# Keys, values and queries as three products of high and low parts in the rounded 32-bit type, single input buffers, a ring of 10 rows

## What is computed

```python
q = layernorm(x) @ Wq + bq;  k = ctx @ Wk + bk;  v = ctx @ Wv + bv
qp = elu(q) + 1;  kp = elu(k) + 1
# causal: sums over s <= t of kp[s] (outer) v[s], times qp[t], for each head
out = (cumulated(kp v) . qp) / cumsum(qp, axis=1)
x = x + out @ Wo + bo
h = relu(layernorm(x) @ W1 + b1);  sel = argmax(h @ W2 + b2)
x = x + layernorm(x) @ expert_W[sel] + expert_b[sel]
```

## Time and profile before

| | |
|---|---|
| time, median of 3 runs | 1251.42 us (1249.2 to 1252.38) |
| span of the profiled execution | 1101.6 us |
| the profiled execution's own time | not given apart from its span; the median is 149.8 us longer than the span |
| PE, DVE, POOL, ACT busy | 1010.6, 879.8, 672.5, 374.5 us |
| one full step | 30.70 us |

### The profile page before, as it was taken

How to read it: one execution, slowest core, us unless ns; L and a number is a source line. 1 busy time by engine, 2 the same in 40 slices (tenths; PEclk the granted TensorE clock), 3 DMA queues, 4 the chain that set the end, 5 groups by cost and what they waited for, 6 DMA issues and landing times.

```text
span 1101.6 us, 37703 instructions
## 1 busy us (share of the span) xinstructions
PE 1010.6 (92%) x15724; PEld 723.6 (66%) x15724; DVE 879.8 (80%) x1908; ACT 374.5 (34%) x581; POOL 672.5 (61%) x578
## 2 busy tenths in 40 slices
PE   1869999999999999999999999999999999997683
PEld 1446666666777776776677777776676767776472
DVE  2468888998988988888988888888998888885552
ACT  0323333333333343343333333344333333331220
POOL 5134556555666666677666666677766566565755
PEclk9979999999999999999999999999999999998887
DMA  4743434444455445555555544445555544351451
GB/s 139 232 113 101 125 121 125 126 128 145 130 163 160 137 121 145 153 150 164 137 153 163 158 120 126 152 150 163 144 148 165 151 120 128 102 151 41 160 174 53
DMA packets 90920, 152.52 MB, mean 138 GB/s; under 512 B 19325, under 2 KB 57856, under 8 KB 90624
## 3 DMA queue, kind: packets, MB, share of 16 engines
q1 hardware_dynamic: 68864, 107.82, 35.3%
q0 software_dynamic: 12672, 33.84, 8.4%
q10 hardware_dynamic: 9216, 8.46, 3.7%
HBM read 98.20 MB, written 36.13 MB: 122 GB/s over the span
## 4 chain that ended last, share of the span: by engine, by line
PE 78%; DVE 8%; issue 4%; DMA 2%; SPq 1%; POOL 0%; ACT 0%; DVEq 0%; POOLq 0%; ACTq 0%
PE b_a L916 23%; PE b_b L921 18%; PE b_s L1006 9%; PE b_b L953 6%; PE b_s L930 6%; PE b_b L963 5%; DVE stage L634 3%; PE b_s L943 3%; PE b_s L971 2%; PE b_a L911 2%; PE b_s L991 2%; DVE kp L783 1%; DVE st L769 1%; DVE vsel L790 1%; DMA out<-rows 1%
## 5 line engine op out<-in xcount | busy, mean ns | idle before, releaser
L634 DVE TENSOR_TENSOR stage<-b_s,causal 128x1024 f32<-128x1024 f32 x192 | 225.5, 1215 | 6.7 <-PE b_s L930 4.2
L466 POOL DMA_INDIRECT out<-rows x136 | 160.3, 1178 | 45.1 <-issue 34.6
L458 POOL DMA_INDIRECT buckets<-row,place x128 | 141.6, 1106 | 34.5 <-issue 34.2
L916 PE MATMUL b_a<-x_T,wq_sb 128*128 128x512 f32 x256 | 128.9, 628 | 18.7 <-POOL x_T L483 14.2
L475 POOL TENSOR_TENSOR onehots<-onehots,onehot 128x32 bf16<-128x32 bf16 x32 | 7.8, 243 | 193.7 <-DVE place L754 193.7
L921 PE MATMUL b_b<-wo_sb,attT 128*128 128x256 f32 x512 | 121.3, 391 | 2.9 <-DVE attT L831 2.9
L916 PE MATMUL b_a<-ctxT,wk_sb 128*128 128x512 f32 x256 | 118.4, 605 | 1.8 <-ACT pos L530 1.8
L921 PE MATMUL b_b<-wv_sb,ctxT 128*128 128x256 f32 x512 | 119.0, 386 | 0.0
L483 POOL TENSOR_TENSOR x_T<-x_T,scale 128x1024 f32<-128x1024 f32 x32 | 75.5, 2360 | 65.6 <-DMA scale<-scales 64.8
L1006 PE MATMUL b_s<-we_sb,x3T 128*128 x464 | 113.2, 389 | 1.0 <-ACT x3T L539 1.0
L497 POOL TENSOR_TENSOR x_res<-x_res,bias_o 128x1024 f32<-128x1024 f32 x32 | 105.8, 3305 | 5.7 <-DMA x_res<-in_x 5.5
(11 more groups left out here) (125 smaller groups left out, 1794.2 us busy)
## 6 DMA issues: line engine op xcount, KB each, us to landing
rows<-buckets SPq DMA_DIRECT2D x136, 130.0 KB
x_in<-in_x SPq DMA_DIRECT2D x32, 512.0 KB, 4.1
x_T<-in_xT SPq DMA_DIRECT2D x32, 512.0 KB, 4.0
ctxT<-in_ctx SPq DMA_DIRECT2D x32, 512.0 KB, 4.6
qsel<-qp SPq DMA_DIRECT2D x256, 64.0 KB, 2.4
x_res<-in_x SPq DMA_DIRECT2D x32, 512.0 KB
scale<-scales ACTq DMA_DIRECT2D x32, 256.0 KB, 3.9
out<-rows POOLq DMA_INDIRECT x136, 3.4
```

The source lines that it names most:

```text
L458: pool.indirect_dma_start(buckets, bass.IndirectOffsetOnAxis(place[:, slot(route), t:t + 1], 0), row[:, slot(route), t, :], None).then_inc ...
L466: pool.indirect_dma_start(out.rearrange("t p n -> (t p) n"), bass.IndirectOffsetOnAxis(rows2[:, r, TOKEN:TOKEN + 1].bitcast(U32), 0), rows ...
L634: dve.tensor_tensor(dst.rearrange("p g h s q -> p g (h s) q"), b_s[:, :, 256 * t:256 * t + 256].rearrange("p g (a q) -> p g a q", q=C), ca ...
L916: last = pe.matmul(dst, w[:, k, P * h:P * h + P], rows[:, k, :], start=(k == 0), stop=(k == KC - 1))
```

## The change

The weights Wq (after its mean is taken out), Wk and Wv, the scaled x_T and ctxT are each split into a high part, the value rounded to float32r by an ACT copy, and a low part, the value minus the high part, also rounded. Each product becomes three: high x high, high x low, low x high. The low parts of x_T and ctxT are made by POOL, those of the weights once by DVE. To make room, x_in, x_res and ctxT have one buffer, attT and x2n share one, the plain weights lie in `stage` until they are split, and the ring of rows has 10 places instead of 15. The diff, cut to its core:

```diff
-    RING = 15
+    RING = 10
...
-    MADE = 13
+    MADE = 19
...
+        wq_parts = [sb(f"wq_{part}", [P, KC, D], F32R) for part in ("high", "low")]
...
-        x_in = sb("x_in", [P, 2, GT, D])
-        x_res = sb("x_res", [P, 2, GT, D])
-        ctxT = sb("ctxT", [P, 2, KC, N])
+        x_in = sb("x_in", [P, GT, D])
+        x_res = sb("x_res", [P, GT, D])
+        ctxT = sb("ctxT", [P, KC, N])
+        ctx_parts = [sb(f"ctx_{part}", [P, KC, N], F32R) for part in ("high", "low")]
...
+        x_parts = [sb(f"x_{part}", [P, KC, N], F32R) for part in ("high", "low")]
...
-        attT = sb("attT", [P, KC, N])
+        att_or_x2n = sb("att_or_x2n", [P, KC * N])
...
+        wq_sb, wk_sb, wv_sb = (stage[:, KC * D * i:KC * D * (i + 1)].rearrange("p (k n) -> p k n", k=KC) for i in range(3))
...
@@ sync: step
-                    if group_no(load) >= 2:
-                        sp.wait_ge(s_st1, n(load, 4, -4))
+                    if group_no(load) >= 1:
+                        sp.wait_ge(s_st1, n(load, 4))
...
-                    if group_no(norm) >= 2:
-                        sp.wait_ge(s_v, n(norm, 2, -2))
+                    if group_no(norm) >= 1:
+                        sp.wait_ge(s_clow, n(norm))
...
-                        sp.wait_ge(s_x1, added)
+                        sp.wait_ge(s_x1, n(attend, 2))
...
-                        sp.wait_ge(s_q, n(load, 2))
+                        sp.wait_ge(s_xlow, n(load))
...
@@ gpsimd
+            def x_low(norm):
+                pool.wait_ge(s_xhigh, n(norm, k=1))
+                if group_no(norm) >= 1:
+                    pool.wait_ge(s_q, n(norm, 2))
+                pool.tensor_tensor(x_parts[1][:, :, :], x_T[:, :, :], x_parts[0][:, :, :], ALU.subtract).then_inc(s_xlow, 1)
...
                     pool.tensor_tensor(z[:, :], z[:, :], u[:, :], ALU.mult).then_inc(s_zprod, 1)
+                    if norm:
+                        x_low(norm)
...
                     pool.tensor_tensor(rstd1[:, :], ve1[:, :], column(neg_half), ALU.pow).then_inc(s_rstd1, 1)
+                if norm:
+                    pool.wait_ge(s_chigh, n(norm, k=1))
+                    pool.tensor_tensor(ctx_parts[1][:, :, :], ctxT[:, :, :], ctx_parts[0][:, :, :], ALU.subtract)\
+                        .then_inc(s_clow, 1)
...
@@ scalar
+            for parts, w in ((wk_parts, wk_sb), (wv_parts, wv_sb)):
+                act.activation(parts[0][:, :, :], w, ACT.Copy).then_inc(s_whigh, 1)
+            act.wait_ge(s_cst, MADE - 6)
+            act.activation(wq_parts[0][:, :, :], wq_sb, ACT.Copy).then_inc(s_whigh, 1)
...
+                if norm:
+                    act.wait_ge(s_xs, n(norm, k=1))
+                    if group_no(norm) >= 1:
+                        act.wait_ge(s_q, n(norm, 2))
+                    act.activation(x_parts[0][:, :, :], x_T[:, :, :], ACT.Copy).then_inc(s_xhigh, 1)
                 turn_out(extra_slots_of(j))
...
                     first_queries(norm, 1)
+                    act.wait_ge(s_ctx[slot(norm)], 16 * half(norm) + 16)
+                    if group_no(norm) >= 1:
+                        act.wait_ge(s_v, n(norm, 2))
+                    act.activation(ctx_parts[0][:, :, :], ctxT[:, :, :], ACT.Copy).then_inc(s_chigh, 1)
...
@@ vector
+            for at, (parts, w) in enumerate(((wk_parts, wk_sb), (wv_parts, wv_sb), (wq_parts, wq_sb))):
+                dve.wait_ge(s_whigh, at + 1)
+                for k in range(KC):
+                    dve.tensor_tensor(parts[1][:, k, :], w[:, k, :], parts[0][:, k, :], ALU.subtract).then_inc(s_cst, 1)
             dve.wait_ge(s_cst, MADE)
...
@@ tensor
+            def pairs_of_parts(weights, rows):
+                for k in range(KC):
+                    for a, b in ((0, 0), (0, 1), (1, 0)):
+                        yield weights[a][:, k, :], rows[b][:, k, :], k == 0 and a + b == 0, k == KC - 1 and a == 1
+            def channels_first_parts(dst, weights, rows, h):
+                for w, r, start, stop in pairs_of_parts(weights, rows):
+                    last = pe.matmul(dst, w[:, P * h:P * h + P], r, start=start, stop=stop)
+                return last
...
-                    pe.wait_ge(s_ctx[a], 16 * half(project) + 16)
+                    pe.wait_ge(s_clow, n(project, k=1))
                     pe.wait_ge(s_qe, n(project, 4, 4))
-                    channels_first(b_a[:, 0, :], wk_sb, ctxT[:, a, :, :], 0).then_inc(s_k, 1)
+                    channels_first_parts(b_a[:, 0, :], wk_parts, ctx_parts, 0).then_inc(s_k, 1)
...
-                        last = tokens_first(b_b[:, t // 2, D * (t % 2):D * (t % 2) + D], ctxT[:, a, :, :], wv_sb, t)
+                        last = tokens_first_parts(b_b[:, t // 2, D * (t % 2):D * (t % 2) + D], ctx_parts, wv_parts, t)
...
-                    pe.wait_ge(s_xs, n(norm, k=1))
+                    pe.wait_ge(s_xlow, n(norm, k=1))
...
-                    channels_first(b_a[:, 0, :], wq_sb, x_T, 0).then_inc(s_q, 1)
+                    channels_first_parts(b_a[:, 0, :], wq_parts, x_parts, 0).then_inc(s_q, 1)
```

More of the change, by code:

```diff
@@ L5 @@
 F32 = mybir.dt.float32
+F32R = mybir.dt.float32r
 BF16 = mybir.dt.bfloat16
@@ L485, in step @@
                                        ALU.mult).then_inc(s_xs, 1)
+                if norm and not attend:
+                    x_low(norm)
                 if merge and j < STEPS - 2:
@@ L817, in step @@
                     for t in range(GT):
-                        dve.bn_stats(st1[:, t, :], x_in[:, slot(load), t, :]).then_inc(s_st1, 1)
+                        dve.bn_stats(st1[:, t, :], x_in[:, t, :]).then_inc(s_st1, 1)
                     aggregate1(load)
```

42 lines of the change are left out of this document (25 added, 17 removed).

## The result

| | before | after |
|---|---|---|
| time, median | 1250.47 us (1249.2 to 1252.38, 4 runs) | 1265.23 us (1259.85 to 1275.29, 4 runs) |
| ratio | | 1.0131, 95% interval 1.0081 to 1.018 |
| profiled execution: its time, its span | span 1101.6 | 1269.16, 1267.4 |

The account below looks back on a forecast made before the run. PE was taken to bound the steps, with a POOL and DVE loop closing after the change. Steps +7 - 3, fill +10 and tail +31 gave +45, 1296 us, rounded down to 1294; range 1263 to 1335.

Parts of the forecast that it names:

- +7 - 3 = +4: Steps: 24 full ones +0.3 us each, +7; six or so earlier ones gain about 0.5 each, -3.
- so I set the sum against the span and take what lies around it as unchanged: Starting point: 149.8 us of the 1251.42 us median lie around the 1101.6 us profiled span and stay unchanged.
- (a): Rival: POOL's path is shorter, PE's gain arrives in full, 28.0 us steps, 1211 us, 5%; half the gain, 1261, 5%.
- (d): Rival: the shorter ring doesn't slow the tail, as its loads are covered; 1263 us, 4%.
- POOL's loop: Steps: POOL's list with two subtractions, closed through DVE from onehots to onehots, takes 30.8 to 31.2 us against 30.70.
- PE's 2.8 us a step: Projections on PE: rounded products at a quarter price give 2.8 us less work a step, which turns into waits.
- x_res without the scan in its way: POOL in a step: x_res, reached 3 us later, no longer meets the DVE scan and takes 2.36 us, not 3.62.
- Fill +10: Before the first rank product: weight parts on DVE +2.7 us, copies and subtractions before first queries and keys +6.8, together +10.
- Tail +31: Tail with ring of 10: +8 us from loads delaying the pad stores, +23 from five of seven quads waiting.
- first pair of products 1.75: Tail: PE's first pair of products priced at 1.75 us, half of 3.49, within 9.8 us a quad.
- (b): Rival: a POOL subtraction costs like x_res, 3.6 us, lengthening the loop by 2.4 us more; 1363 us, 12%.
- (c): Rival: rounded products cost half of a 32-bit product on PE, +5.6 us a step; 1420 us, 4%.

Follow-up runs that it names:

- the ring alone: Kernel before with a ring of 10 rows instead of 15 and nothing else; 1146.47 us, ratio 1.0374.
- high parts alone: Changed kernel with only the high x high product, low parts of x and context neither made nor multiplied; 1107.09 us, repeated at 1103.73.
- half of the late sums: Kernel before with late sums over the first half of the positions only; 1081.01 us, ratio 0.9777, repeated at 1079.37.
- the queries first: Kernel before with the first half of the queries ahead of the first late sums on PE; 1116.85 us, ratio 1.0094.
- Single buffers (+2.1%): Kernel before with one buffer each for x_in, x_res and ctxT, nothing else changed; 1276.24 us, ratio 1.0209.
- plain products: Changed kernel with all its splitting, but one plain 32-bit product of the high parts for each three; 1172.55 us (1.0612) and 1277.83 us (1.0198).

## Why the prediction was wrong, and where it was right

Rank products mark the stages. From their rows (first and last start) and the spans:

| | first rank product | from first to last | to the end |
|---|---|---|---|
| forecast | +10 | +7 - 3 = +4 | +31 |
| first kind (109.2, 927.7, 69.7 to 114.8, 938.8, 108.7) | +5.6 | +11.1 | +39.0 |
| second kind (105.7, 1060.0, 80.9 to 116.1, 1037.9, 113.4) | +10.4 | **-22.1** | +32.5 |

**The step that failed** is "so I set the sum against the span and take what lies around it as unchanged". Nothing but 1.7 us lies around the span. The profiled execution and the timed runs were made, as far as the spans tell, on two kinds of chip, and on the one that was timed the steps take 36 us, not 30.70. There the working starts from a wrong bound: PE's work stretched by pauses among its small products, 5.2 us a step. From the first rank product to the last the change saves 22 us there, where the forecast had +4. The same block averages, before against after, show of what: a step falls from 36.3 to 34.4 us. The small products take 1.0 us less (early scores -1.0, late sums -3.8, early sums +3.7), keys, values and queries 2.2 less, of which 1.2 is in the first queries, and PE waits 1.0 longer ahead of the late sums, for vsel. So the pauses moved more than they shrank, and PE's cheaper projections, which the forecast saw turn into waits, show here in part. Fill and tail came near the forecast, +43 together against +41. In sum the traces have +20.8 us (1267.4 - 1246.6), the medians +14.8, the forecast +45. It is luck that 1265 lies in the range and beside the times of two rivals, the half of (a) at 1261 and (d) at 1263: (d) has the tail unchanged, which it isn't, and the half of (a) counts from steps of 30.7 us without pauses. A gap of 12% between span and median called for a rival of its own: that the timed runs have other steps than the profiled one.

**On the kind of chip that the rows came from, most of the working held.** Its sum was +45, measured +58 by the medians (1162.61 - 1104.32), +55.7 by the traces. Not shown is that POOL's loop alone sets the steps: with x_low taken out of it they stayed at 31.5 us, on a chain through DVE and PE. Point by point there:

- Rounded products at a quarter: right, a start every 0.23 us for 512 columns. The forecast's sign of being wrong, "records of the rounded products over 0.25 us", would have misled: the records last 0.40 us and overlap. PE's 2.8 us a step: PE's busy time fell from 30.52 to about 29, not to 28; the gain went into waits, as forecast, some of them for vsel, which the forecast took to be there in time (29.3 us over the run).
- ctx_low at 2.46: 2.36 measured. x_low at 2.46 behind kp: mean 2.77, as it waits for kp's end.
- Steps of 30.8 to 31.2: 31.0 to 31.3 in those without a table, 31.9 in those with one. On the mean of steps 12 to 25 it is 31.6 against 31.1 in the kernel before, +0.5 instead of +0.3. The term is too small, and what the rows show beside it is the second query sum, which x_res now meets; the forecast had "x_res without the scan in its way" and did not follow whom it meets in its new place.
- POOL's idle ahead of onehots "from 6 to about 2 us": 2.22.
- Fill +10: +5.6 on this kind, +10.4 on the other.
- Tail +31: +37.7 by the ring alone. The two parts were +8 and +23; measured, the first of the 28 blocks is sent 31.0 us after the last rank product (1068.79 - 1037.8) instead of 24.2, +6.8, and the 28 take 67.1 instead of 35.5 us, +31.6. The largest miss is in "first pair of products 1.75": 3.0 to 3.4 with part of it at the lower clock. A turn takes 11 us instead of 9.8, and the first two 13.6 and 11.8.
- Single buffers at nothing: agrees with the sum of the first kind; not isolated there.

**The rivals.** (a), which the sentence on the passes calls the second rival, falls on the first kind: its steps are longer, not shorter, and the high parts alone show that even 8.4 us less of PE's work than before give only 1.6 us a step. (b) and (c) by the rows of x_low and L966. (d) by the run of the ring alone.

**Open.** What the pauses are. They come with the kind of chip and not with one kernel: idle stretches of PE over 0.3 us by "issue", from the first to the last rank product, number 136 (58.9 us) in the kernel before and 143 (62.2 us) in the changed one on the second kind, and 6 in each on the first. Nearly all lie in stretches of small products, 0.4 us each at a spacing of 0.75. The Trainium skill (Runtime: NRT & Kernel Launch, Instruction fetch mechanics) says that a sequencer fetches its instructions ahead in blocks of 16 KiB and that crossing one is mostly hidden. The page of the profile agrees on the blocks (queue q8: 129 packets, 2.11 MB), and they take about the same share of time on both kinds, 0.7 and 0.8%. Of the 126 pauses among the late and early sums of the kernel before on the second kind, 28 overlap one of the 125 block transfers; by chance it would be some 18 (an estimate from their lengths and the span). So most pauses aren't the block transfers themselves, and whether PE runs short of instructions at all isn't shown. Three edits were meant to tell whether the number of instructions or their place counts (half of the late sums, twice, the queries first, high parts alone); all these runs fell on the first kind. Single buffers (+2.1%) and plain products (+2.0%) show only that they go by more than the number of instructions.

## What to carry to other kernels

Compare the span of a profile with the timed median before anything is worked out from its rows; when they differ by much more than the 1.7 us of these runs, the bound that the rows show need not be the bound of the runs. When a bound engine is relieved, add up the next one with every instruction of another engine that it has to wait for: here DVE's busy time stood 3 to 5 us a step behind PE's (27.7 with a table, 25.8 without, against 30.5), and POOL's two new two-input instructions, with x_res moved by them, stretched DVE's query sums by 2.3 us a step, nearly all of the 2.8 us that PE gained. Follow every closed path between the engines, and not only the one through the engine that got new work: here one through DVE and PE was as long. A shorter ring costs once for every quad whose loads wait, five of seven here, and in such a tail PE's products are to be priced with a lower granted clock (0.71 to 0.84).

## What the runs showed of the hardware

- Two kinds of chip: the same program takes 1106 us on three chips and 1250 us on two others and in the first comparison, in 43 and 24 runs of the kernel before that stood beside the others, with nothing between 1113.21 and 1244.35. In the steps the difference lies in stretches of small products with pauses of PE of 0.4 us, 5.2 us of a step.
- A product of two float32r operands takes 0.23 us for 512 columns and 0.12 for 256 from start to start, about 1.1 cycles a column at the 2.4 GHz level, a quarter of a 32-bit product.
- In these rows DVE and POOL instructions with two inputs in SBUF run one after the other, whichever started first (x_res 3.62 us instead of 2.36 on POOL, L683 2.43 and 3.35 instead of 0.68 on DVE). It holds for small ones: "tied" of 128x32 took 1.46 us instead of 0.20 beside a subtraction on POOL. "logits", of the same size but with one input in PSUM, took its 0.19 us beside the same subtraction.
